# Time mixing: the denominators' reciprocal taken by a logarithm, an exponential and one Newton step

## The reference

```
qt  = maximum(pp, kt + u)
e1  = exp(pp - qt);  e2 = exp(kt + u - qt)
out = (e1 * aa + e2 * vt) / (e1 * bb + e2)
pp_new = maximum(pp + neg_ew, kt)
aa, bb = f1 * aa + f2 * vt, f1 * bb + f2
```

## Time and profile before

| | |
|---|---|
| median of the runs | 853.4 us |
| profiled execution, its own time | 852.91 us |
| span of the profile | 851.2 us |
| PE busy in the span | 649.4 us |
| DVE busy | 541.4 us |
| ACT busy | 342.6 us |
| POOL busy | 327.1 us |

### The profile page before, as it was taken

One profiled execution on the slowest core, in us unless ns is written; L12 is line 12 of the kernel. 1 busy time (PEld: TensorE's weight loads), 2 busy tenths in 40 slices (PEclk: granted clock), 3 DMA queues, 4 the chain that ended last, 5 costly groups with the idle time before them and its releaser, 6 DMA issues. The chain is left out here.

```text
span 851.2 us, 14119 instructions
## 1 busy us (share of the span) xinstructions
PE 649.4 (76%) x4265; PEld 534.9 (63%) x4265; DVE 541.4 (64%) x1122; ACT 342.6 (40%) x760; POOL 327.1 (38%) x306
## 2 busy tenths in 40 slices
PE   4989999669916999999944899999344069999600
PEld 3656665358815888888833788888344048888400
DVE  4578989626782556444421799998556748888433
ACT  1567777324402333333315566544045025555200
POOL 5877764000003343434314466634310043331075
PEclk9999999969967999999986999999755569999855
DMA  4000000045303111111106000000059023332154
GB/s 124 1 2 1 2 2 2 3 149 189 95 1 87 52 56 57 57 57 50 50 25 198 1 1 1 2 0 1 0 180 307 8 67 98 99 100 81 50 152 138
DMA packets 38466, 54.23 MB, mean 64 GB/s; under 512 B 7252, under 2 KB 30422, under 8 KB 38262
## 3 DMA queue, kind: packets, MB, share of 16 engines
q1 hardware_dynamic: 31624, 34.80, 12.7%
q0 software_dynamic: 6768, 18.49, 7.3%
HBM read 37.28 MB, written 15.99 MB: 63 GB/s over the span
## 5 line engine op out<-in xcount | busy, mean ns | idle before, releaser
L1611 PE MATMUL banks<-r_xt,r_w_mixed 128*128 128x256 f32 x384 | 86.6, 385 | 1.4 <-ACT r_xt L1679 1.4
L1611 PEld LDWEIGHTS banks<-r_xt,r_w_mixed 128*128 128x128 f32 x384 | 73.1, 192 | 12.4 <-ACT r_xt L1679 2.1
L1357 DVE SCALAR_TENSOR_TENSOR f0x_s<-f0x_th,banks 128x512 f32<-128x512 f32 x35 | 24.1, 689 | 82.7 <-ACT f0x_th L1316 78.0
L1219 POOL DMA_INDIRECT f_y<-f0x_yout,f_slot_of x35 | 34.4, 983 | 102.1 <-ACT f0x_yout L1335 99.9
L1205 POOL DMA_INDIRECT f1x_xg<-f_xn,f_token_of x39 | 37.0, 948 | 75.5 <-PE banks L1256 50.9
L568 DVE TENSOR_REDUCE a_ssum<-a_e 128x6 f32<-128x1536 f32 x32 | 56.0, 1749 | 2.7 <-ACT a_e L454 2.5
L1272 PE MATMUL banks<-f_w_hi,f0x_xt_hi 128*128 x140 | 56.1, 401 | 0.2 <-issue 0.2
L1316 ACT ACTIVATE f0x_th<-banks 128x512 f32<-128x512 f32 x35 | 20.9, 598 | 86.5 <-PE banks L1272 86.5
L1272 PE MATMUL banks<-f_w_hi,f0x_xt_lo 128*128 x140 | 55.6, 397 | 0.0
L1272 PE MATMUL banks<-f_w_lo,f0x_xt_hi 128*128 x140 | 55.3, 395 | 0.0
L454 ACT ACTIVATE a_e<-banks 128x1536 f32<-128x1536 f32 x32 | 46.5, 1455 | 15.8 <-PE banks L351 15.8
(11 more groups left out here) (330 smaller groups left out, 1889.0 us busy)
## 6 DMA issues: line engine op xcount, KB each, us to landing
f_y<-f1x_yout SPq DMA_DIRECT2D x39, 128.0 KB
f0r_stage<-in_f_w13T SPq DMA_DIRECT2D x4, 1024.0 KB
r_y<-f_y SPq DMA_DIRECT2D x16, 256.0 KB, 6.0
f1r_stage<-in_f_w13T SPq DMA_DIRECT2D x8, 512.0 KB
f0r_stage<-in_f_w2T SPq DMA_DIRECT2D x4, 512.0 KB
f_xn<-f0r_xn SPq DMA_DIRECT2D x8, 256.0 KB
f1r_stage<-in_f_w2T SPq DMA_DIRECT2D x8, 256.0 KB
f_xn<-f1r_xn SPq DMA_DIRECT2D x8, 256.0 KB
```

The source lines that it names most:

```text
L1219: pool.indirect_dma_start(k.y_dram, bass.IndirectOffsetOnAxis(ap=k.slot_of[:, t:t + 1], axis=0), yout[:, t % YB, :], None).then_inc(scatte ...
L1611: last = pe.matmul(bank(1 + kind)[:, eb * T:(eb + 1) * T], r.w_mixed[:, kind, j // KB, j % KB, eb * P:(eb + 1) * P], xt[:, b % 2, j % KB, ...
```

## The change

DVE's reciprocal goes. A new step `invert(b)` on ACT takes the logarithm of `den` and then the exponential of its negative, which is a first guess g of 1/den. A new step `quotient(b)` on DVE takes one Newton step, g(2 - den g), in two operations, and multiplies it with `num` in a third. The steps are placed anew: `invert(b-1)` is first in iteration b, and `quotient(b-1)` stands behind `scores(b)`, with `centre(b-1)` behind it. After the loop both run once more for the last batch.

```diff
         for b in range(B):
+            if b > 0:
+                w.invert(b - 1)
             if b + 1 < B:
                 front(b + 1)
+            w.scores(b)
             if b > 0:
+                w.quotient(b - 1)
                 w.centre(b - 1)
-            w.scores(b)
             if b > 0:
                 w.square(b - 1)
...
-        for step in (w.centre, w.square, w.gate, w.shift, w.add_shift, w.project, w.deviate, w.vary, w.add):
+        for step in (w.invert, w.quotient, w.centre, w.square, w.gate, w.shift, w.add_shift, w.project, w.deviate, w.vary, w.add):
...
+            def invert(self, b):
+                act.wait_ge(done["den_done"], b + 1)
+                act.activation(log_den[:], den[:], ACT.Ln).then_inc(done["log_done"], 1)
+                act.wait_ge(done["log_done"], b + 1)
+                at_least(act, done["less_two"], b)
+                act.activation(guess[:], log_den[:], ACT.Exp, scale=-1.0).then_inc(done["guess_done"], 1)
...
+                at_least(dve, done["missed"], b)
                 then(dve.tensor_tensor(den[:], ex[:, 0], ab[:, 1, :, 0:T], ALU.mult), "e1b_done")
-                then(dve.tensor_tensor(den[:], den[:], ex[:, 1], ALU.add), "den_done")
-                then(dve.reciprocal(rden[:], den[:]), "rden_done")
+                dve.tensor_tensor(den[:], den[:], ex[:, 1], ALU.add).then_inc(done["den_done"], 1)
+
+            def quotient(self, b):
+                dve.wait_ge(done["guess_done"], b + 1)
+                dve.tensor_tensor(miss[:], den[:], guess[:], ALU.mult).then_inc(done["missed"], 1)
+                dve.wait_ge(done["missed"], b + 1)
+                dve.scalar_tensor_tensor(out=miss[:], in0=miss[:], scalar=2.0, in1=guess[:], op0=ALU.subtract,
+                                         op1=ALU.mult).then_inc(done["less_two"], 1)
+                dve.wait_ge(done["less_two"], b + 1)
                 dve.wait_ge(done["num_done"], b + 1)
                 at_least(dve, done["centred"], b)
-                dve.tensor_tensor(wkv[:], num[:], rden[:], ALU.mult).then_inc(done["wkv_done"], 1)
+                dve.scalar_tensor_tensor(out=wkv[:], in0=miss[:], scalar=-1.0, in1=num[:], op0=ALU.mult,
+                                         op1=ALU.mult).then_inc(done["wkv_done"], 1)
```

More of the change, by code:

```diff
@@ L1483, in rwkv_phase @@
     dif, rel, ex = sb("dif", [P, EB, T]), sb("rel", [P, 2, EB, T]), sb("ex", [P, 2, EB, T])
-    e2v, e1a, num, den, rden, wkv, sq, rw = (
-        sb(n, [P, EB, T]) for n in ("e2v", "e1a", "num", "den", "rden", "wkv", "sq", "rw"))
+    e2v, e1a, num, den, log_den, guess, miss, wkv, sq, rw = (
+        sb(n, [P, EB, T]) for n in ("e2v", "e1a", "num", "den", "log_den", "guess", "miss", "wkv", "sq", "rw"))
     ve, rstd = sb("ve", [P, S]), sb("rstd", [P, S])
@@ L1489, in rwkv_phase @@
              "top_done less_done sc_done dif_done rel_done ex_done f2v_done e2v_done scan_done e1a_done num_done "
-             "e1b_done den_done rden_done wkv_done centred sq_done rw_done shifted shift_added var_done ve_done rstd_done "
+             "e1b_done den_done log_done guess_done missed less_two wkv_done centred sq_done rw_done shifted shift_added var_done ve_done rstd_done "
              "out_done x_done bn_done aggr_done eps_done next_rstd")
@@ L1573, in divide, with invert, quotient @@
         def divide(self, b): pass
+        def invert(self, b): pass
+        def quotient(self, b): pass
         def centre(self, b): pass
```

## The result

The changed kernel takes 910.97 us, the median of four runs (909.78 to 911.13), against 853.38 us for the one before: a ratio of 1.067, with a 95% interval of 1.065 to 1.069. The forecast was 910, the range 890 to 932. The span went from 851.2 to 908.1 us.

A forecast was written before the change was run, and what follows sets the result against it. TensorE was taken to set the pace, with 2.85 us of slack for the quotient. Five periods 40.0, first batch 6.0, last iteration 8.8 and tail 1.9 sum to 56.7 us, on 852.9 giving 909.6, rounded to 910; range 890 to 932.

The forecast's parts named there:

- Part 2 and 3: ScalarE: inversion waits behind the copy of v (offset 11.26); two table loads per batch; guess ready at 15.12.
- The open point: Cost of one ScalarE table load on the path: 1.28 us taken, 2.66 kept for the upper end.
- Part 4: VectorE and TensorE: scores end at 13.27, guess decides, centring starts at 17.4; period 25.05 us against 17.05.
- my figure for e3: Time mixing without loads: scores decide, TensorE waits about 4.4 us or less, clock stays up; 885 us (882 to 890).
- The clock: TensorE's centring: a 6.3 us hole, longer than 4.1, drops the clock to 1.2 GHz; 1.39 us per period.
- five full periods: From the start of products(2) to that of products(7): 8.0 us more each, 40.0 in all.
- no loads: Rival for ScalarE: all functions share one table, scores decide, clock holds; period 21.8, total 887 us; chance 0.06.
- first period: First batch: the scores' end at 488.95 decides, products(2) start at 498.8 against 492.85; 6.0 us more.
- products(7) to its `den`: Last iteration, without next products: 29.0 us against 20.2, slow centring included; 8.8 more.
- `den` to the last centring: Tail: two loads, logarithm, exponential and quotient make 6.1 us against 4.2; 1.9 more.

The follow-up runs named there:

- e1: The kernel before, reciprocal kept on VectorE, with only the product (and the centring behind it) moved behind the next scores; 871.13 us, ratio 1.022.
- e7: The changed kernel with a table holding logarithm and exponential named ahead of the logarithm, so the second load falls ahead of the tangent; 901.44 us, ratio 1.057.
- e3: The changed kernel with the logarithm replaced by a square, so no table loads and an output that isn't the reference's; 894.64 us, ratio 1.050.
- e9: The changed kernel with 12 idle matmuls ahead of TensorE's wait for the quotient, in seven of eight batches; 896.03 us, ratio 1.052.
- e5: The changed kernel with the inversion moved up on ScalarE, between the gate's tangent and the copy of k, quotient still behind the scores; 888.02 us, ratio 1.042.
- e6: As e5, with the quotient and the centring also put ahead of the next scores; 864.85 us, ratio 1.015.
- e8: The kernel before with VectorE's statistics put behind the next scores instead of ahead of them; 852.59 us, ratio 1.001.
- e10: As e8, and the gate of the batch before put ahead of the gap on VectorE; 852.37 us, ratio 0.999.

## Why the prediction was right

**What bounds the kernel.** TensorE set the pace, and its in-order queue with the centring at its head was the place to look at. e1 shows this best: a product moved on an engine with slack, nothing added, 19 us. VectorE's 2.1 us per batch were saved (16.1 to 16.2 us, 13.5 to 14.7 in the full periods after) and bought nothing in any run.

**Part 2 and 3, ScalarE.** The guess at 563.62 - 548.48 = 15.14 (15.12 forecast), two loads of 1.28 us in each inversion, logarithm and exponential 0.63 us. The open point, 1.28 or 2.66 us for a load, is settled by rows: the logarithm starts at 561.04, straight behind the load's end at 561.03. By the Trainium skill, ScalarE: Activation LUTs, section What ACT_TABLE_LOAD costs, 1.38 us more should follow each; this trace has none of it, in the middle of the stream, which fits the DMA that the earlier trace rows names for that wait. The Trainium skill's 1283 ns for the load itself agree with the 1.28 us here. The Trainium skill's other rule, ScalarE: Activation LUTs, section Table sets: the hidden batching unit, one load for a logarithm followed by an exponential, holds only where the table is named (e7: one load ahead of the pair), not as the change is written (two).

**Part 4, the order.** The scores end at 560.63 - 548.48 = 12.15, not at 13.3 as I had left them; VectorE, relieved, comes to them sooner. As the guess was later anyway, it cost the forecast nothing, though it made my figure for e3 rest on the wrong wait.

**The clock.** The mechanism holds (e9). Its size was too small: 1.39 us per period was the price where the clock comes back behind the centring, as in the earlier trace rows. Three of the five full periods have that (25.1 us). In the other two (26.2 us) it came back only late in the shift (at about 545.2 in the one whose centring starts at 539.67), and they cost 1.1 us more. Where I failed is the condition. I took 4.1 us without matmuls, from one hole, as what it takes. In the changed kernel the clock fell 2.8 us after the last matmul (562.3 - 559.5) and in the next period 5.0 us after it (589.6 - 584.6). e3 lost it in holes of 3.6 us; e5 lost it in one of 2.99 and kept it in one of 3.42; e1 lost it with one wait of 2.33 us and kept it with two others of the same length. How long a hole must be isn't a fixed number in these runs. My price for "no loads", 887, was therefore too low, and it didn't even follow from my own figure: its hole was 15.5 - 11.06 = 4.4 us, longer than 4.1, and I priced its periods with the clock up. The kernel made so took 894.6.

**The sum, term by term.**

| term | forecast | measured |
|---|---|---|
| five full periods | 40.0 | 127.55 - 85.23 = 42.3 |
| first period | 6.0 | 27.15 - 20.38 = 6.8 |
| products(7) to its `den` | 8.8 | 29.36 - 20.23 = 9.1 |
| `den` to the last centring | 1.9 | 4.84 - 4.17 = 0.7 |
| before and behind these | 0 | -2.0 |
| span | 56.7 | 56.9 |

So the hit within 1 us is partly luck: the clock's late return in two of the five full periods (+2.3) and in the first period (+0.8) is set off by the tail (-1.2) and by a time mixing that began 2.4 us earlier, which isn't of the change's making: over all traces of this case its first products start anywhere from 456.67 to 459.86. The tail was cheaper because of something I hadn't seen:

```profile
649.62 1.28 ACT L1713 ACT_TABLE_LOAD   x1
...
653.42 0.69 DVE L1786 TENSOR_TENSOR r_den<-r_den,r_ex 128x512 f32<-128x512 f32 x1
...
654.14 0.63 ACT L1713 ACTIVATE r_log_den<-r_den 128x512 f32<-128x512 f32 x1 [3.24 <-DVE r_den L1786]
```

The load stands ahead of the wait for `den`, not behind it, so the last logarithm's load is hidden.

**Shares.** Undoing one thing at a time is worth: the inversion's place 21 us, the loads 14, the second load's place 9, the clock 13, VectorE's order 0; together with the earlier inversion, VectorE's order is worth 24 more (1.042 to 1.015). They don't sum to 57, as each removes a wait behind which the next one stands.

## What to carry to other kernels

Before freeing an engine, ask whether its work is on the path, and how long the result lay ready before the engine that needs it came for it; here it was 2.85 us, and that is all that a detour over two other queues may cost. A step that goes to another engine takes its place in that engine's order: put it straight behind what makes its input (e5, 21 us for moving one call). And when the engine that sets the pace gets a hole of a few us, count the slower clock behind it besides the hole.

## What the runs showed of the hardware

- A table load in the middle of ScalarE's stream is 1.28 us and nothing more: in the changed kernel 0.01 to 0.02 us lie between an activation and the load behind it, and as much between the load and the next activation.
- A load that the program didn't name stands ahead of its activation's semaphore wait, and is hidden if the wait is long: in the last batch of the changed kernel it began at 649.62, and the wait ended at 654.14. The load named by hand behind the wait stays behind it: in e7's last batch it began at 648.13, straight behind the denominator.
- TensorE's clock fell with holes of 6.3 us and of 3.6 us (e3) each time, with 2.33 us once in three (e1), and never with 1.2 us (e6); in e5 it fell with 2.99 us and not with 3.42. It stayed at the 1.2 GHz level for 3 to 6 us of work. Twelve idle matmuls, 5.35 us, in each of seven holes made the kernel 13 us faster.
- In e8, and in e10 too, the first scores behind the move ran beside GpSimd's addition to x, and one of their scans took 1.75 us, where the longest of the sixteen in the kernel before took 0.69. That the addition is the cause is read from the overlap alone; the 1.1 us lost are some of what the reordering could have won there:

```profile
L1743 DVE TENSOR_TENSOR_SCAN r_kt<-r_grown,r_kt x14: 659/671/1751, 483.4 to 587.4; 128x256 f32<-128x256 f32 x14
```
